# A perceiver block's last stage: two weight splits and one normalisation moved later on ScalarE, and eight copies moved from VectorE to ScalarE

## What is computed

```python
x = x + cross_attention(context, layernorm(x), mask, ...)
x = x + self_attention(layernorm(x), Qw, Kw, Vw)
y = layernorm(x)
for l in range(2):
    h = shift_token(y)
    q, k, v = split(h @ wqkv[l])              # 8 heads of 64
    q, k = rotary(l2norm(q) * qs, l2norm(k) * ks)
    y = y + local_attention(q, k, v) @ wo[l]  # window of 128
    a, g = split(layernorm(shift_token(y)) @ w1[l] + b1[l])
    y = y + (a * gelu(g)) @ w2[l] + b2[l]
x = x + y
```

## Time and profile before

| | us |
|---|---|
| median of 3 runs (1059.42 to 1062.51) | 1061.09 |
| the profiled execution's own time | 1058.91 |
| its span in the trace | 1057.1 |
| transformer stage and its prologue, from about 700 us of the span to its end | 357 |

### The profile page before, as it was taken

The page is one execution under the profiler, slowest core; times in us unless marked ns, Lnnn a source line. Parts: engine busy times, 40 slices in busy tenths (PEclk is TensorE's granted clock), DMA queues, the critical chain, the costliest instruction groups (busy, mean ns, idle before and its releaser), DMA issues. The chain is left out here.

```text
span 1057.1 us, 25664 instructions
## 1 busy us (share of the span) xinstructions
PE 1014.4 (96%) x8683; PEld 942.2 (89%) x8684; DVE 814.4 (77%) x3009; ACT 664.2 (63%) x1542; POOL 205.1 (19%) x265
## 2 busy tenths in 40 slices
PE   6999999999999999999999998988999999999997
PEld 5899999999999999999999998966878989889887
DVE  6887777695877786877786787589988889889753
ACT  4865665674655665566565556576676776767753
POOL 0111111110111111111111111360006203263213
PEclk9999999999999999999999999999999999999999
DMA  6000000000000000000000100510010000010000
GB/s 203 23 12 3 10 1 1 11 12 4 11 2 0 11 13 3 12 2 0 11 13 2 34 2 2 186 17 2 1 41 21 2 1 21 25 58 2 1 22 21
DMA packets 28804, 21.64 MB, mean 20 GB/s; under 512 B 12095, under 2 KB 26268, under 8 KB 28700
## 3 DMA queue, kind: packets, MB, share of 16 engines
q1 hardware_dynamic: 28529, 20.21, 6.5%
q10 hardware_dynamic: 170, 0.07, 0.0%
HBM read 19.17 MB, written 1.05 MB: 19 GB/s over the span
## 5 line engine op out<-in xcount | busy, mean ns | idle before, releaser
L302 PEld LDWEIGHTS pv_ps<-v,pt 128*128 128x128 f32 x1792 | 214.9, 192 | 9.5 <-issue 3.0
L302 PE MATMUL pv_ps<-v,pt 128*128 128x65 f32 x1792 | 215.2, 272 | 3.3 <-DVE o L817 1.9
L795 DVE CUSTOM_DVE_ANT_0 s_sb<-s_ps,pen,mstate 128x256 f32<-128x256 f32 (+1 forms) x512 | 199.9, 446 | 13.9 <-issue 11.0
L509 ACT ACTIVATE probs<-s_sb,mbias 128x256 f32<-128x256 f32 (+1 forms) x512 | 203.2, 470 | 0.0
L669 POOL TENSOR_TENSOR o<-o,alpha 128x260 f32<-128x260 f32 x128 | 85.9, 671 | 561.8 <-ACT alpha L503 561.8
L518 ACT ACTIVATE pt<-turn 128x512 f32<-128x512 f32 x128 | 76.3, 596 | 122.9 <-PE turn L289 109.0
L289 PE MATMUL turn<-ident,probs 128*128 128x128 f32 x896 | 123.8, 278 | 0.1
L289 PEld LDWEIGHTS turn<-ident,probs 128*128 128x128 f32 x896 | 98.8, 144 | 9.5 <-issue 0.3
L817 DVE TENSOR_TENSOR o<-o,pv_ps 128x260 f32<-128x260 f32 x128 | 54.0, 422 | 46.1 <-PE pv_ps L302 34.9
L278 PE MATMUL s_ps<-kh,qh 64*128 64x256 f32 (+1 forms) x512 | 78.8, 304 | 2.8 <-DVE x L839 1.5
L767 DVE TENSOR_TENSOR kl<-proj,kh 128x512 fp32r<-128x512 f32 (+1 forms) x63 | 41.3, 655 | 51.6 <-ACT kh L496 51.0
(11 more groups left out here) (431 smaller groups left out, 2732.0 us busy)
## 6 DMA issues: line engine op xcount, KB each, us to landing
raw<-in_ctx SPq DMA_DIRECT2D x24, 128.0 KB, 2.1
f_wqkv_raw<-in_L_ffn_wqkv SPq DMA_DIRECT2D x6, 512.0 KB, 5.2
f_w_raw<-in_L_ffn_w SPq DMA_DIRECT2D x8, 256.0 KB, 4.9
f_w_raw<-in_L_ffn_w SPq DMA_DIRECT2D x2, 640.0 KB
wkv_raw<-in_L_xattn_Wkv SPq DMA_DIRECT2D x1, 1024.0 KB, 6.8
wout_raw<-in_L_xattn_Wout SPq DMA_DIRECT2D x1, 1024.0 KB, 11.0
f_wo_raw<-in_L_ffn_wo SPq DMA_DIRECT2D x2, 512.0 KB, 4.5
x<-in_x SPq DMA_DIRECT2D x1, 768.0 KB, 8.7
```

Of the source, the lines that this page charges most:

```text
L302: last = pe.matmul(t.pv_ps[:, u, :], t.pt[g % 2][:, u, kt, :], t.v[:, kt, h, :], start=(kt == 0), stop=(kt == kts - 1))
L509: last = act.activation(t.probs[g % 2][:, u, 0:kts * P], t.s_sb[g % 2][:, u, 0:kts * P], ACT.Exp, bias=t.mbias[:, at:at + 1], scale=0.125)
L795: last = dve.tensor_tensor_reduce(out=t.s_sb[g % 2][:, u, 0:width], in0=t.s_ps[g % 2][:, u, 0:width], in1=t.pen[:, 0:width], scale=1.0, sc ...
```

## The change

Three edits of ScalarE's stream, the third of which also takes copies out of VectorE's. No other engine's stream is touched:

1. `high_piece` of w12 and w2 goes from ahead of iteration 0 to a place within it, behind the last `heads_hi` and ahead of `first_deviations`.
2. The `first_normed` of the last four tiles (units 2 and 3) goes from the end of iteration 0 into iteration 1, behind the exponentials of unit 0's pair 2, head 0.
3. For units 0 and 1, ScalarE's `store_turned` copies head 1 as well, behind its copy of head 0, and VectorE's returns at once: eight copies (two units of four pairs). The semaphores keep their names and counts. The second copy waits for the transposition of head 1.

```diff
--- before.py
+++ after.py
@@ -50,6 +50,7 @@
 COUNT_AT = SLOT_AT + PAIRS + 1
 PLAN = COUNT_AT + 2
 FINISH_BUFFER = (0, 1, 1, 0)
+COPIED_BY_ONE = (0, 1)
 
 LH, LDH, LI = 8, 64, 512
 HID = 682
@@ -1808,6 +1809,9 @@
                 if at:
                     act.wait_ge(s["pv_done"], at)
                 act.activation(t.pt[0][:].rearrange("p k q -> p (k q)"), t.turn[0][:, 0:3 * P], ACT.Copy).then_inc(s["pt_act"], 1)
+                if u in COPIED_BY_ONE:
+                    act.wait_ge(s["t_done_odd"], at + 1)
+                    act.activation(t.pt[1][:].rearrange("p k q -> p (k q)"), t.turn[1][:, 0:3 * P], ACT.Copy).then_inc(s["pt_dve"], 1)
 
             def output_hi(u, q, bank):
                 act.wait_ge(s["o_turned"], count(2, u, q))
@@ -1927,8 +1931,6 @@
             store_tile(0, 1, 1, t.g[2])
             squares(0, 1)
             first_normed(3, range(QT, 2 * QT))
-            high_piece(act, s, ("w12", first["w12"]))
-            high_piece(act, s, ("w2", first["w2"]))
             for T in range(0, UNITS + 1):
                 if valid(T - 1):
                     exponentials(T - 1, 1, 1)
@@ -1940,6 +1942,8 @@
                     hidden_hi(T - 3, 5)
                 if valid(T - 1):
                     exponentials(T - 1, 2, 0)
+                if T == 1:
+                    first_normed(5, range(2 * QT, TILES))
                 if valid(T - 2):
                     deviations(T - 2)
                 if valid(T):
@@ -1969,6 +1973,8 @@
                 if valid(T):
                     heads_hi(T, 1, 1, t.g[2])
                 if T == 0:
+                    high_piece(act, s, ("w12", first["w12"]))
+                    high_piece(act, s, ("w2", first["w2"]))
                     first_deviations(4, slice(2 * QT, TILES))
                 if valid(T + 1):
                     store_tile(T + 1, 0, 1, t.g[1])
@@ -2012,8 +2018,6 @@
                     hidden_hi(T - 2, 4)
                 if valid(T + 1):
                     squares(T + 1, 1)
-                if T == 0:
-                    first_normed(5, range(2 * QT, TILES))
             output_hi(LAST, 1, t.s[0])
             gelu(LAST - 1, 1, t.g[1])
             hidden_hi(LAST - 1, 0)
@@ -2104,6 +2108,8 @@
                                          ).then_inc(s["bias_ready"], 1)
 
             def store_turned(u, p):
+                if u in COPIED_BY_ONE:
+                    return
                 at = PAIRS_OF * u + p
                 dve.wait_ge(s["t_done_odd"], at + 1)
                 if at:
```

## The result

| | before | after |
|---|---|---|
| median of 6 runs of each | 1060.80 us | 1054.47 us (1053.19 to 1055.98) |
| ratio, with its 95% interval | | 0.9935 (0.9921 to 0.9950) |
| the profiled execution's own time | 1058.91 us | 1054.65 us |
| its span | 1057.1 us | 1052.8 us |

The changed kernel is faster by 0.65% by the ratio (6.9 us), and by 6.3 us between the two medians. The forecast was 1056.9 us with a range of 1054.0 to 1060.5: the result lies in the range, near its lower end, and the gain is more than the 4.2 us of the sum. Between the two profiled executions the difference is 4.26 us. So there are two things to explain: whether the 4.2 us came from where the prediction had them, and where the other 2 us are.

What follows compares the result with a forecast made beforehand. The fill's chain of semaphore waits was taken to set the time, its gains passed on to the end. 3.9 + 0.3 = 4.2 us less took the profiled 1058.91 to 1054.7 and the median 1061.09 to 1056.9 us, range 1054.0 to 1060.5.

Steps and rivals of the forecast that it cites:

- the sum: Whole kernel: 3.9 us from the fill and iteration 1 plus 0.3 us from iteration 2, 4.2 us less.
- Edit 1, taken away: In the fill, without weight copies and with VectorE not held, `rotate_sum` starts at 709.8: lead 4.2 us.
- Edit 1, put back: Copies hide in ScalarE's idle time; GpSimd holds `f_bias` 1.6 us more, the product behind 0.6; lead 2.7 us at `f_sums_raw`.
- The second collision: In the fill, the small offsets product behind `f_bias` meets GpSimd's last instruction (42x256), costing 0.6 us.
- Edit 2: At the seam of iterations 0 and 1, exponentials of pair 1, head 1 start at 727.9, not 732.66: lead 4.8 us.
- TensorE's wait of 1.91 us goes, and with it the lower clock: At the seam, scores, transposes and head transposes in 733.7 to 737.2 each take some 0.4 to 0.7 us less.
- Edit 3: Copies gain nothing in iteration 1, where VectorE waits for ScalarE, and give 0.3 us in iteration 2.
- the transfer to the median: Profiled execution lies 2.2 us under the median of 1061.09; the same difference taken from that median gives 1056.9 us.
- Round trips: In iteration 1, second copies hold ScalarE for head 1's transposition; lead shrinks by 1.5 to 2.7 us: 1058.4 us; chance 0.25.
- The collision misses: In the fill, `f_bias` and the product behind it pass GpSimd; 5.5 us less, 1055.6 us; chance 0.12.
- The steady iterations take it back: GpSimd and VectorE meet at other instants, or second-layer weights decide; some 0.5 us left, 1060.6 us; chance 0.06.
- TensorE at the lower clock in all of iteration 1: Gaps of 1.5, 1.3 and 1.0 us lower the clock from 729 to 739; 3.0 us slower, 1064.1 us; chance 0.07.

Runs made afterwards that it cites:

- n1: Changed kernel with the weight copies earlier on ScalarE and GpSimd waiting for VectorE's scaling of unit 0's second-half keys: 1054.17 us, ratio 0.9933.
- e4_no_copies: Changed kernel without ScalarE's eight second copies, the other two edits kept: 1054.78 us, ratio 0.9946.
- e1_weights: Kernel before with only the `high_piece` calls of w12 and w2 moved into iteration 0: 1057.01 us, ratio 0.9965.
- n2_split_tiles: Changed kernel with unit 2's two tiles left in place and unit 3's moved behind the squares later in iteration 1: 1053.43 us, ratio 0.9930.
- n3_both: Changed kernel with earlier weight copies, GpSimd waiting for the key scaling, and the four tiles split: 1053.57 us, ratio 0.9921; repeated, 1052.99 us, 0.9924.
- e5_before: Kernel before, nothing changed, run again as a control: 1060.60 us, ratio 0.9995.
- e3_copies: Kernel before with only the eight copies moved from VectorE to ScalarE in units 0 and 1: 1061.58 us, ratio 1.0003.
- f1: Kernel before with 16 matmuls of unused result filling TensorE's 1.91 us wait at the seam: 1060.59 us, ratio 0.9988.
- e2: Kernel before with only the last four normalised tiles moved into iteration 1: 1059.66 us, ratio 0.9990.
- f2: Changed kernel with 8 matmuls of unused result in TensorE's 0.97 us gap ahead of pair 2's transposes: 1055.66 us, ratio 0.9944.

## Why the prediction was right, and where it was wrong

**Edit 1, taken away: right.** `rotate_sum` leads by 4.3 us, forecast 4.2, from the two causes named, the copies out of the path and VectorE no longer held. Edit 1 alone is worth 3.7 us, the largest part.

**Edit 1, put back: right in kind.** The copies are hidden by ScalarE's idle time. `f_bias` took 1.76 us, exactly the 0.16 + 1.6 that its due time within the 2.89 us instruction gave, and more than the longest of the trace of before (1.62). The Trainium skill (SBUF — State Buffer, the two separate sides) says that the blocked engine waits for the whole instruction of the other; `f_bias` ended with GpSimd's long instruction, and n1 with no instruction of GpSimd beside it has 0.16 us, so the runs agree for this instruction. (`f_sums` was stretched too, 0.88 us for 0.17, though it has one tensor input, where the prediction's sentence on the shared ports speaks of two.) The second collision, 0.6 us for the offsets product, didn't happen: that product started at 719.21, as GpSimd's last instruction did, and took 0.15 us; which of the two was first the trace doesn't tell. This is most of the 0.75 us by which the lead of 3.45 exceeds 2.7.

**Edit 2: right.** TensorE's wait for the exponentials is gone, and `wq_hi` behind the tiles leads by 5.0 us (4.2 forecast). On top of edit 1 it gives 1.6 to 2.0 us (e4_no_copies less e1_weights, in the lead at unit 2 and in the medians). Alone it has its 1.9 us at unit 2, and in its profiled execution keeps 0.8 at unit 3 and 0.5 at unit 4, since the clock falls one gap later.

**"TensorE's wait of 1.91 us goes, and with it the lower clock": the second half was wrong.** The clock at 727.5 to 731.5 was full, but it fell at 733, behind gaps that I had thought too short: those of 0.89 and 0.97 us. It cost the trace little, since before had the same at 0.54. n2_split_tiles and n3_both, whose seam is at full clock, lead by 0.9 and 2.3 us more at unit 2; how much of it is this no run separates.

**Edit 3: right.** No gain in iteration 1, where the copies stand in ScalarE's full line; the second copies never waited. The 0.3 us of iteration 2 shows as the gap ahead of `f_z`, 0.46 us shorter in every execution with the copies. The medians can't tell it from nothing, and it no more than makes up for iteration 1: e4_no_copies, without the second copies, leads by 4.66 us at unit 4, after by 4.35. Part of VectorE's freed time turned into waits: in after it waits at 760.49 for 0.71 us, in place of 0.25, and at 771.52 for 0.56, where before it had no wait.

**The sum: right for the fill, and by luck for the whole.** The lead is 3.84 us at unit 2's first projection (forecast 3.9) and 4.35 at unit 4 (4.2). That the profiled execution of after then has 1054.65 us, where 4.2 us gave 1054.7, is in part luck: 0.8 us of the lead was lost to the clock at 935, and the 0.70 us by which this execution was early ahead of every edit made up for it.

**The step that failed: the transfer to the median.** "It lies 2.2 us under the median of 1061.09, from which the same difference gives 1056.9 us." The same difference does not hold for the median: that is 1060.80 - 1054.47 = 6.3 us. The profiled execution of before had an unusual amount of full clock (0.995, the typical run 0.990), and I took those 2.2 us for something that both kernels have. They are not: after's profiled execution lies within 0.2 us of its median. In e5_before (0.989, 2.4 us above the median of its runs, where that of before was 1.9 below) the lower clock behind the same wait lasts some seven microseconds longer and costs 2.4 us, in e3_copies it does so behind the first wait. The changed kernel spends less time at it (0.9953 in the mean, 0.9938 in the repeat). The change took away both long gaps, and with them, as the traces suggest, time at the lower clock of which the profiled execution of before had the least. In the terms of the sum, it is the term for the clock at the seam that was too small: it was taken from one execution, and the others without the change had more to lose. The rows gave a sign: 0.54 behind the wait, 0.71 behind the one of 2.84 us. I priced the first at 0.4 to 0.7 us per group of matmuls, as if it always ended at 737, and did not ask how such a stretch differs between executions. That the range still held the result is luck: its lower end was made of the missed collision and of the spread of the runs, not of this.

**The rivals.** *Round trips* (0.25): not so; before the eight second copies ScalarE never waits, and in the seam its single wait (0.60 us at 734.41) is ahead of a first copy. (The upper end of its price was also added up too high: three times 0.86 is 2.6, not 2.7.) *The collision misses* (0.12): not so, but n1 shows what it would be worth, 0.7 to 1.0 us in the trace and not the 1.5 I had put; the next wait for ScalarE (0.69) takes the other part. *The steady iterations take it back* (0.06): not so: between 814 and 897 us no lead changes by more than 0.03 us. What is lost is lost to the clock at 935. *TensorE at the lower clock in all of iteration 1* (0.07): not so; TensorE's gaps there were 0.84, 0.89 and 0.97 us, not 1.0 to 1.5, and the clock fell for about 3 us, as in before. The time 1054.47 is nearest to the number of the missed collision, for a reason that isn't that rival's.

**What stays open.** That before's profiled execution was 1.9 us faster than its kernel's median is measured. That these 2 us are the clock's is argued from where the 14 traces have the lower clock, from the table of the 59 runs and from the clocks of the parts; no run held the clock fixed, and f1, the one kernel made to test it, kept the seam at full clock and gained 1 us where 1.5 to 3 were expected. Why the clock falls behind one gap in one execution and not behind the same gap in the next (1.69 us at 935, 1.37 at 769) is not settled; f1 and e2 only show a fall at the next gap where the seam has none, and f2 that filling the last gap may leave it where it was. Whether the changed kernel has less of the lower clock because both long gaps are gone, or for another reason, is likewise only argued.

## What to carry to other kernels

Before a difference read from one profiled execution is applied to the median, compare the two: where the execution is faster than the median and its granted clock is higher than that of the other runs, look behind the longest waits of TensorE for the missing time; a change that removes such a wait may win that too. And compare what two executions lose where nothing was changed, here 0.8 us at 935: a sum that comes out to a tenth can hide two errors that cancel. Work of GpSimd that is moved away from one collision with VectorE can meet another, as `f_bias` was met here: compute which instruction is due in its middle, and what that one's followers wait for anyway. Time freed on an engine is worth looking up at its next wait; if that wait is for another engine, the freed time ends there. Here it came through once, as 0.46 us at one gap of TensorE.

## What the runs showed of the hardware that was not expected

- In after, a fall to the lower clock (0.54 in 732.9 to 736.5) stood behind gaps of no more than 0.97 us, and it came with that gap filled too (f2), while a gap of 1.36 us at 769 in before had none behind it.
- What two executions of the same kernel lose in one place can differ by more than the edit studied: the changed kernel lost 0.8 us behind unit 4 in one and 2.4 in another (4.35 to 3.58, 4.41 to 1.99).
- The time at the lower clock behind one and the same wait (1.91 and 1.92 us) differs from execution to execution of one kernel: some 3 us in before's, 10 in e5_before's, which makes 2.4 us in the time of the kernel. Behind the first wait (2.84 us) it was 3 us in four executions and 10 in e3_copies.
- Filling a gap of 1.91 us with matmuls kept the clock full there and let it fall 35 us later (0.66 in 765 to 780, where before had 1.00), in the one execution of it that was traced.
- A VectorE instruction of 128x4 elements, 0.16 us long, took 1.76 us where it met a GpSimd product on 128x1280.
